# q and k of the first eight slots kept as one f32 tile each, their scores as one f32 product per head in row tiles, and the engines' lists of steps laid anew

## What is computed

```
x = x + attention(layernorm(x), Wqkv, Wo)      16 heads of 32, causal, softmax
x = x + ffn(layernorm(x), w1, w3, w2)          hidden size 1365
attention: scores = q k^T / sqrt(32); a = softmax(masked scores); o = a v; o Wo
ffn:       h1 = x w1q^T; h3 = x w3q^T; (silu(h1) * h3) w2q^T
           with wq = clip(round(w / mean|w|), -1, 1) * mean|w|
```

## Time and profile before

| | |
|---|---|
| median of the runs | 579.03 us (578.77 to 580.35, 3 runs) |
| the profiled execution, its own time | 580.78 us |
| its span in the profile | 579.0 us |
| mean granted TensorE clock | 0.941 of full speed |
| PE busy | 508.0 us (88%), 4092 matmuls |
| DVE, POOL, ACT busy | 411.8 us (71%), 368.4 us (64%), 330.2 us (57%) |
| first and last f16 score matmul | 37.1 and 472.8 us |
| scores of slot 5's first fill | 162.4 us |
| last phase (feed-forward of batch 3) | from 515.9 us on |

### The profile page before, as it was taken

How to read it: one execution, slowest core, us unless ns; L and a number is a source line. 1 busy time by engine, 2 the same in 40 slices (tenths; PEclk the granted TensorE clock), 3 DMA queues, 4 the chain that set the end, 5 groups by cost and what they waited for, 6 DMA issues and landing times.

```text
span 579.0 us, 11497 instructions
## 1 busy us (share of the span) xinstructions
PE 508.0 (88%) x4092; PEld 237.9 (41%) x4092; DVE 411.8 (71%) x1026; ACT 330.2 (57%) x833; POOL 368.4 (64%) x460
## 2 busy tenths in 40 slices
PE   2669754857999999999999999999999998839997
PEld 2224322333445444544444444454444454314443
DVE  6599787697899877966888879578878771523421
ACT  4769866777756875645467875363666752012320
POOL 3077689777968976776667887556668782312320
PEclk9689955878999999999999999999999999869999
DMA  8939978999889756387596565675783548030001
GB/s 312 316 30 278 193 170 160 252 200 211 153 141 162 145 124 131 56 158 194 108 167 143 90 131 97 141 180 114 101 173 75 109 87 208 9 63 1 0 37 72
DMA packets 224205, 79.52 MB, mean 137 GB/s; under 512 B 213226, under 2 KB 213226, under 8 KB 224148
## 3 DMA queue, kind: packets, MB, share of 16 engines
q1 hardware_dynamic: 224148, 78.79, 65.0%
HBM read 20.97 MB, written 4.19 MB: 43 GB/s over the span
## 4 chain that ended last, share of the span: by engine, by line
PE 69%; POOL 9%; DMA 8%; SPq 5%; DVE 4%; issue 2%; ACT 2%; DVEq 0%; ACTq 0%
PE work L1120 46%; PE work L1280 13%; DMA early<-early 4%; PE work L1239 4%; PE score_bank L1197 4%; POOL early L654 4%; PE work L1210 2%; DMA rows<-in_L_attn_x 2%; POOL late L687 2%; POOL early L687 1%; SPq L517 1%; DVE early L986 1%; DMA w_ternary<-early 1%; POOL rows L669 1%; DMA late<-rows 1%
## 5 line engine op out<-in xcount | busy, mean ns | idle before, releaser
L654 POOL TENSOR_TENSOR early<-early 128x512 f16<-128x512 f32 (+1 forms) x192 | 193.7, 1021 | 40.4 <-DVE early L986 26.5
L762 ACT ACTIVATE early<-early,exp_bias 128x512 f32<-128x512 f32 (+3 forms) x256 | 140.8, 551 | 76.7 <-POOL exp_bias L661 76.5
L1120 PE MATMUL work<-late,w_ternary 128*128 128x512 f16 (+1 forms) x704 | 158.9, 384 | 10.3 <-DMA late<-rows 10.3
L974 DVE CUSTOM_DVE_ANT_0 early<-score_bank,mask,scalars 128x512 f32<-128x512 f32 (+3 forms) x256 | 131.7, 543 | 32.7 <-POOL early L654 20.4
L986 DVE CAST early<-early 128x512 f16<-128x512 f32 (+1 forms) x148 | 99.5, 690 | 18.1 <-ACT early L762 14.7
L1120 PEld LDWEIGHTS work<-late,w_ternary 128*128 128x128 f16 (+1 forms) x704 | 69.2, 101 | 93.9 <-issue 17.9
L1120 PE MATMUL work<-xt,wqkv_hi 128*128 128x512 f16 x256 | 80.7, 398 | 2.9 <-DVE wqkv_lo L936 2.0
L1280 PE MATMUL work<-w_ternary,late 128*128 128x512 f16 (+1 forms) x352 | 77.7, 379 | 0.0
L679 POOL TENSOR_TENSOR late<-late 128x512 f16<-128x512 f32 (+1 forms) x44 | 51.3, 1168 | 40.1 <-ACT late L799 39.4
L792 ACT ACTIVATE late<-work,scalars 128x512 f32<-128x512 f32 (+1 forms) x44 | 30.0, 682 | 53.0 <-DVE late L1027 36.1
L1120 PE MATMUL work<-xt,wqkv_lo 128*128 128x512 f16 x128 | 51.0, 398 | 0.0
(11 more groups left out here) (103 smaller groups left out, 702.4 us busy)
## 6 DMA issues: line engine op xcount, KB each, us to landing
rows<-in_L_attn_x SPq DMA_DIRECT2D x16, 256.0 KB, 3.0
x_res<-in_L_attn_x SPq DMA_DIRECT2D x12, 256.0 KB, 3.2
out_y<-x_res SPq DMA_DIRECT2D x12, 256.0 KB, 2.8
late<-in_L_ffn_w SPq DMA_DIRECT2D x4, 682.5 KB, 5.5
early<-in_L_ffn_w SPq DMA_DIRECT2D x3, 768.0 KB, 12.8
late<-in_L_ffn_w SPq DMA_DIRECT2D x3, 768.0 KB, 6.7
late<-in_L_attn_Wqkv SPq DMA_DIRECT2D x4, 512.0 KB, 7.2
late<-in_L_attn_Wqkv SPq DMA_DIRECT2D x1, 1024.0 KB, 9.8
```

Source lines behind the costliest of these rows:

```text
L654: pool.tensor_tensor(split_view(s, p, 1, h), raw_view(s, p, h), split_view(s, p, 0, h), ALU.subtract).then_inc(low_done, 1)
L762: last = act.activation(piece, piece, ACT.Exp, bias=bias, accum_out=sums[:, s % 2, at:at + 1])
L974: last = dve.tensor_tensor_reduce(raws[n % RAWS][:, off:off + cols], score_bank[h][:, off:off + cols], mask[:, S - cols:S], scalar(exp_sca ...
L1120: last = pe.matmul(bank, lhs, rhs, start=(n == 0), stop=(n == len(terms) - 1))
```

## The change

For slots 0 to 7 (`WHOLE = 8`) ACT copies q and k once, as f32, into a whole tile; DVE makes no low half of them, and the bank is freed by ACT's copy. `scores` then issues one f32 product per head and piece in place of three f16 ones. The f16 halves of slots 8 to 15 lie in the same memory. `HALF` leaves out the copies without a partner, and `xt` on SP waits for the last reader in each work bank. The core of the diff:

```diff
@@ -42,6 +42,7 @@
 WARM = 4
 HALVES = 3
 RAWS = 4
+WHOLE = 8
 
 
 FILLS = (((3, 0, 512),), ((2, 0, 384), (0, 384, 128)), ((1, 0, 256),))
@@ -264,7 +272,8 @@
 
 
 WORK = numbered("pe", "top_turn", "weight_mean", "xt", "q", "k", "v", "project", "gate", "lin", "down", "inverse", "values")
-HALF = numbered("act", "xt", "yt", "q", "k", "v")
+HALF = {step: n for n, step in enumerate(s for s in ORDER["act"] if s[0] in ("xt", "yt", "v") or
+                                         s[0] in ("q", "k") and s[1] >= WHOLE)}
 HIGHS = {engine: numbered(engine, "high") for engine in ("act", "dve")}
 SPLIT = numbered("act", "split", "wo_split")
 
@@ -334,8 +343,9 @@
 
         v_hi = sb("v_hi", [P, ST, D], F16)
         v_lo = sb("v_lo", [P, ST, D], F16)
-        half = {(n, part_): [sb(f"{n}_{part_}{i}", [P, S], F16) for i in range(HALVES)]
-                for n in "qk" for part_ in ("hi", "lo")}
+        whole = {n: [sb(f"{n}{i}", [P, S], F32) for i in range(HALVES)] for n in "qk"}
+        half = {(n, part_): [w[:, at // 2:(at + S) // 2].bitcast(F16) for w in whole[n]]
+                for n in "qk" for part_, at in (("hi", 0), ("lo", S))}
 
         row_max = sb("row_max", [P, 2, 2 * HG], F32)
         exp_bias = sb("exp_bias", [P, 2, 2 * HG], F32)
@@ -544,8 +554,10 @@
                 kind, b, i = step
                 n = kind[0]
                 if kind == "xt":
-                    for used in [(m, GROUPS * b - 1) for m in "qk"] + [("v", b - 1, j) for j in range(ST)]:
-                        full(sp, used)
+                    readers = [(m, GROUPS * (b - 1) + g) for m in "qk" for g in range(GROUPS)]
+                    readers += [("v", b - 1, j) for j in range(ST)]
+                    for n_bank in range(NW):
+                        full(sp, max((r for r in readers if bank_of(r) == n_bank), key=turn_of))
                     sp.wait_ge(rows_split[n], ST * (b - 1) + i + 1)
                 else:
                     if b:
@@ -742,7 +754,11 @@
                 if s >= HALVES:
                     act.wait_ge(score_full, NF * (s - HALVES + 1))
                 full(act, step)
-                act.activation(half[n, "hi"][s % HALVES][:], work[bank_of(step)][:], ACT.Copy,
+                if s < WHOLE:
+                    act.activation(whole[n][s % HALVES][:], work[bank_of(step)][:], ACT.Copy,
+                                   scale=QK_SHRINK).then_inc(work_free[bank_of(step)], 1)
+                    return
+                act.activation(half[n, "hi"][s % HALVES], work[bank_of(step)][:], ACT.Copy,
                                scale=QK_SHRINK).then_inc(half_done, 1)
 
             def v_high(step):
@@ -952,7 +968,7 @@
                 n, s = step
                 bank = bank_of(step)
                 dve.wait_ge(half_done, HALF[step] + 1)
-                dve.scalar_tensor_tensor(half[n, "lo"][s % HALVES][:], work[bank][:], QK_SHRINK, half[n, "hi"][s % HALVES][:],
+                dve.scalar_tensor_tensor(half[n, "lo"][s % HALVES], work[bank][:], QK_SHRINK, half[n, "hi"][s % HALVES],
                                          ALU.mult, ALU.subtract).then_inc(work_free[bank], 1)
 
             def v_low(step):
@@ -1188,15 +1204,19 @@
                 if p == 0:
                     for n in "qk":
                         emptied(pe, (n, s))
+                at = s % HALVES
+                terms = [(half["q", a][at], half["k", b][at]) for a, b in (("hi", "hi"), ("hi", "lo"), ("lo", "hi"))]
+                if s < WHOLE:
+                    terms = [(whole["q"][at], whole["k"][at])]
                 for j, (tile, off, cols) in enumerate(FILLS[p]):
-                    for t, (a, b) in enumerate((("hi", "hi"), ("hi", "lo"), ("lo", "hi"))):
+                    for t, (q, k) in enumerate(terms):
                         for h in range(HG):
                             if fill and j == t == 0:
                                 pe.wait_ge(score_free, HG * (fill - 1) + h + 1)
                             heads = slice(HD * h, HD * (h + 1))
                             last = pe.matmul(score_bank[h][:, off:off + cols],
-                                             half["q", a][s % HALVES][heads, tile * P:(tile + 1) * P],
-                                             half["k", b][s % HALVES][heads, 0:cols], start=(t == 0), stop=(t == 2))
+                                             q[heads, tile * P:(tile + 1) * P], k[heads, 0:cols],
+                                             start=(t == 0), stop=(t == len(terms) - 1))
                 last.then_inc(score_full, 1)
 
             def inverse_rows(step):
```

All five lists are laid anew. The places of them that the prediction speaks of (lines before with -, lines after with +, cut at the sides by "..."):

```diff
     "sp":
-        x_load:1,1 res_load:0,2 res_load:0,1 x_load:1,0 weight_turn:w1,0 res_load:0,0 weight_turn:w1,1
-        weight_load:w3,0 weight_turn:w1,2 weight_load:w3,1-2 probs_turn:0,0 weight_load:w3,3 probs_turn:0,1 xt:1,0-1
+        x_load:1,0-1 weight_turn:w1,0 weight_load:w3,0-2 weight_turn:w1,1-2 weight_load:w3,3 res_load:0,2
+        probs_turn:0,0-2 xt:1,0-1 x_load:1,2-3 probs_turn:1,0 weight_load:w2,0 probs_turn:1,1 weight_turn:w3,0
     "pool":
-        bias:0,0,3 low:0,0,1-2 bias:0,1,1 low:0,0,3 bias:0,1,3 stats_x:1,1 low:0,1,0-3 bias:0,2,1 xt:1,0 low:0,2,0
-        bias:0,2,3 low:0,2,1-2 xt:1,1 bias:1,0,1 low:0,2,3 bias:1,0,3 low:1,0,0-2 bias:1,1,1 low:1,0,3 stats_x:1,2
-        bias:1,1,3 low:1,1,0-1 xt:1,2 stats_x:1,3 low:1,1,2-3 weight_round:w3,0 bias:1,2,1 weight_round:w3,1
+        low:0,0,2 bias:0,1,1 low:0,0,3 bias:0,1,3 low:0,1,0-2 bias:0,2,1 low:0,1,3 stats_x:1,1 low:0,2,0 bias:0,2,3
+        weight_round:w3,0 low:0,2,1-2 bias:1,0,1 low:0,2,3 weight_round:w3,1-2 xt:1,1 bias:1,0,3 low:1,0,0-1
+        weight_round:w3,3 low:1,0,2 bias:1,1,1 weight_round:w3,4 low:1,0,3 stats_x:1,2 weight_round:w3,5 bias:1,1,3
     "act":
-        split:2 weight_sum:w1,3 split:3 split:8 split:4 k:0 q:0 weight_ternary:w1,0 split:5 weight_ternary:w1,1-2
+        weight_sum:w1,2 split:2 weight_sum:w1,3 split:3 norm_x:1,0 split:8 weight_ternary:w1,0 k:0
+        weight_ternary:w1,1 q:0 split:4 weight_ternary:w1,2 split:5 weight_ternary:w1,3 split:6 weight_ternary:w1,4
     "dve":
-        pad:w1 stats_x:0,0-3 top_part:0-1 xt:0,0 top_part:2-3 xt:0,2-3 top_turn:qk top_v split:0 xt:0,1 top_turn:v
-        split:1 stats_x:1,0 split:2-3 weight_mean:w1 split:8 q:0 split:4 k:0 wo_max max:0,0,0 split:5 max:0,0,1
-        split:6 q:1 max:0,0,2 high:0,0,0 max:0,0,3 split:7 high:0,0,1 q:2 max:0,1,0 high:0,0,2 max:0,1,1 high:0,0,3
+        pad:w1 stats_x:0,0-3 top_part:0-3 xt:0,1 xt:0,0 xt:0,2 top_turn:qk xt:0,3 split:0 top_v stats_x:1,0 split:1
+        top_turn:v weight_mean:w1 wo_max split:2-3 split:8 split:4 max:0,0,0 split:5 max:0,0,1 split:6-7 v:0,0
+        max:0,0,2-3 high:0,0,0-1 top_turn:wo high:0,0,2 max:0,1,0-1 high:0,0,3 pad:w3 max:0,1,2-3 v:0,1 high:0,1,0-1
     "pe":
-        lin:2,10 values:14 down:2,0 scores:15,2 down:2,1-2 inverse:15 down:2,3 values:15 project:3,0-3 gate:3,0-1
+        values:14 scores:15,2 down:2,0-2 inverse:15 values:15 down:2,3 project:3,0-3 gate:3,0-1 lin:3,0-1 gate:3,2-3
```

More of the change, by code:

```diff
@@ L130 @@
+        low:14,1,0 lin:2,4 low:14,1,1-2 bias:14,2,1 low:14,1,3 lin:2,5 bias:14,2,3 low:14,2,0-2 lin:2,6 bias:15,0,1
+        low:14,2,3 bias:15,0,3 lin:2,7 low:15,0,0 lin:2,8 low:15,0,1-3 bias:15,1,1 lin:2,9 ot:13 bias:15,1,3
+        low:15,1,0 lin:2,10 low:15,1,1-2 bias:15,2,1 low:15,1,3 bias:15,2,3 low:15,2,0-3 ot:14-15 stats_y:3,0-1
+        yt:3,0-1 stats_y:3,2-3 yt:3,2-3 lin:3,0-10
     """,
     "act": """
-        norm_x:0,0-2 xt:0,0 norm_x:0,3 xt:0,1-3 weight_sum:w1,0 split:0 weight_sum:w1,1 split:1 weight_sum:w1,2
@@ new lines @@
+        stats_x:3,1 down:0,0 max:8,0,0 inverse:7 max:8,0,1-3 q:10 high:8,0,0-2 max:8,1,0 high:8,0,3 down:0,1
+        max:8,1,1-2 down:0,2 values:7 high:8,1,0 max:8,1,3 high:8,1,2 down:0,3 high:8,1,1 high:8,1,3 project:1,0
+        stats_y:1,0 max:8,2,0-1 project:1,1 max:8,2,2 stats_y:1,1 max:8,2,3 norm_y:1,0-1 v:2,0 project:1,2 max:9,0,0
+        stats_y:1,2 max:9,0,1-2 project:1,3 high:9,0,0 max:9,0,3 norm_y:1,2 stats_y:1,3 high:9,0,1 q:11 inverse:8
+        max:9,1,0 norm_y:1,3 max:9,1,1 high:9,0,2 v:2,1 high:9,0,3 k:11 max:9,1,2 v:2,2 max:9,1,3 v:2,3 high:9,1,0
@@ new lines @@
+        high:11,0,1 inverse:10 q:12 high:11,0,2 gate:1,10 max:11,1,0 q:13 max:11,1,1 lin:1,10 high:11,0,3 max:11,1,2
+        k:12 max:11,1,3 high:11,1,1 high:11,1,0 values:10 max:11,2,0 high:11,1,2 max:11,2,1 high:11,1,3 max:11,2,2
+        k:13 max:11,2,3 down:1,0 inverse:11 max:12,0,0 down:1,1 max:12,0,1-3 high:12,0,0-1 down:1,2 high:12,0,2
+        max:12,1,0 values:11 max:12,1,1-2 high:12,0,3 high:12,1,0 down:1,3 max:12,1,3 high:12,1,1 project:2,0
+        max:12,2,0 stats_y:2,0 high:12,1,2-3 max:12,2,1-2 project:2,1 norm_y:2,0 max:12,2,3 stats_y:2,1 project:2,2
@@ new lines @@
+        high:14,1,0 gate:2,5 high:14,1,1 lin:2,5 max:14,2,0 high:14,1,2 values:13 max:14,2,1 high:14,1,3 gate:2,6
+        lin:2,6 max:14,2,2-3 gate:2,7 lin:2,7 max:15,0,0-1 inverse:14 max:15,0,2 gate:2,8 max:15,0,3 lin:2,8
```

(18 more changed lines are left out.)

259 lines of the change are left out of this document (116 added, 143 removed).

## The result

The change makes the kernel slower by 0.3 to 0.6 per cent: 581.85 us median (580.74 to 583.15) against 580.01 us (577.64 to 580.65), eight runs each, ratio 1.0046 with a 95% interval of 1.003 to 1.0063. The ratios here are not the quotients of the medians, which can differ from them by some 0.1%. Run again beside other kernels it gave 581.66 us, 1.005 (1.0032 to 1.0067). The forecast, 570.8 us, had the wrong sign, and its range (562 to 579) does not hold the result.

A forecast was written before the change was run, and what follows sets the result against it. It saw a front of waits between four engines, a stretch bound by TensorE's matmuls, and an end with a stall. Terms -2.0 + 1.9 - 3.5 - 4.6 = -8.2 us gave 570.8 us against the median, range 562 to 579.

The forecast's parts named there:

- start -2.0: Start: x_load 1,0 issued first and w1's mean read earlier, so w1's rounding begins about 2.0 us earlier; first scores at 34 us.
- front -3.5: Front up to scores 5,0: less DVE work plus DMA room used, less the late w1 turn (1 us), gives -3.5 us.
- f32 +0.5: Front's f32 score fills: +2.9 us of matmuls, of which 0.5 us was put on the path.
- +1.4: Eight f32 score fills in the saturated stretch (5,1 to 7,2): four tiles abreast, 4/3 of the passes, +1.4 us.
- -4.6: End: down 2,3 behind values 15 removes the 2.85 us ot_lo stall and 1.7 us of half clock: -4.6 us.
- the price put on DVE's time: Front: of 9.5 us less DVE work, at most a third, 2 to 3 us, reaches a waiting engine.
- Rival 3: Front is held by DMA and POOL whatever DVE does; the last 3.5 us do not come, 574.5 us; 20%.
- the 2.5 us for the new order's use of DMA: Front: w3 loads issued earlier, while DMA has room, gain about 2.5 us net of the residual loads.
- Rival 4: Front loses: late w1 turn or new POOL list delays biases; front +3 instead of -5.5, 579 us or more; 11%.
- The mark: TensorE time of a 512-column f32 fill: 0.9 to 1.0 us forecast, 2.1 shows rival 2, 3.4 rival 1.
- rivals 1 and 2: f32 row tiles run one at a time (592 us, 7%), or half overlapped, two heads' records together (579 us, 6%).
- moved waits on SP cost nothing: SP's moved waits of xt cost nothing, as TensorE is past those matmuls in both orders.

The follow-up runs named there:

- e3: Kernel before with its lists, DVE's q and k steps of slots 0 to 7 struck out, three products of hi halves alone: 578.41 us, 0.9996.
- e2: Changed kernel with its own lists, but scores of slots 0 to 7 as three f16 products of hi halves, no f32: 582.17 us, 1.0063.
- e4: Kernel before with only down 2,3 moved behind values 15 on TensorE, its DVE step ahead of project 3,0: 577.05 us, 0.997.
- e7: Changed kernel with first scores ahead of q:1 on TensorE and split 1 ahead of the statistics of x 1,0 on DVE: 581.82 us, 1.0055.
- e12: Changed kernel with two low halves of v moved up on DVE: 581.38 us, 1.0039.
- e6: Changed kernel with w1's three turns on SP ahead of the first three w3 loads: 585.34 us, 1.0108.
- e1: Changed kernel's f32 product on the engine lists of the kernel before, DVE's q and k steps of slots 0 to 7 struck out: 582.47 us, 1.007.
- e8: Lists of the kernel before with the end of e4, f32 product for slots 0 to 4 only (WHOLE = 5): 578.45 us, 0.9981.
- e10: e8 with f32 for all eight slots (WHOLE = 8), DVE's q and k steps of slots 5 to 7 struck out: 580.18 us, 1.0017.
- e5: Changed kernel with batch 0's turned rows of y ahead of slot 4's last probability turn and xt 2,0 on SP: 583.12 us, 1.0057.
- e9: Changed kernel with w2's last two chunks rounded, signed and turned earlier, and e5's order on SP: 582.33 us, 1.0066.

## Why the prediction was wrong

**The prediction's sum, against the balance.** Both are counted against the profiled execution of before.

| stretch | predicted | profiled |
|---|---|---|
| up to scores 5,0 | -5.0 (start -2.0, front -3.5, f32 +0.5) | +1.9 (matmuls +4.1, lost -2.3) |
| f32 fills after it | +1.4 | +2.5 |
| new wait, scores 5,0 to 6,0 | none | +2.6 lost |
| scores 6,0 to 15,0 | none | -1.0 lost |
| end up to gate 3,0 | -4.6 | -3.4 lost |
| after gate 3,0 | none | -1.3 lost |
| sum | -8.2 | +1.3 |

**The failed step is the front's -3.5**, both of its gains. The first is the price put on DVE's time, 2 to 3 us. The prediction read 20.6 us of waits for row_max as a sign that a third of DVE's saved time would reach a waiting engine. e3 shows that none does, within 1.3 us. A wait names who came last. It does not say that this engine's own work was what the others were short of. Rival 3 (20%), by which the front does not care what DVE does, was right on that; its time, 574.5 us, failed with the other terms. The second is the 2.5 us for the new order's use of DMA: by medians the new lists without their end cost an estimated 5.8 us when there is no f32 product (3.8 of e2 less e3, and e4's 2.0), of which about 3 us lie at gate 0,0 (below) and the rest in the front.

**The front's new order costs instead of giving.** From the chain of the changed kernel's whole span:

```profile
48.77 3.11 SPq L614
...
51.93 3.81 DMA w_ternary<-early
...
55.75 8.55 DMA early<-early
...
82.85 5.01 POOL early L666 x4
...
87.93 6.29 SPq L580
...
94.26 2.09 SPq L614
...
106.10 8.45 DMA early<-early
```

w1 is turned at 55.7 us (53.2 before, forecast 54 to 55), and the first probability turn lands at 64.3 us. That is not earlier than before: the piece of the earlier trace rows that ends at 69.5 us is two turns. DVE's cast behind the first one starts, in the kernel before and then in the changed one, at

```profile
61.21 0.29 DVE L986 CAST early<-early 128x256 f16<-128x256 f32 x1 [0.27 <-DMA early<-early]
```

```profile
64.32 0.29 DVE L1002 CAST early<-early 128x256 f16<-128x256 f32 x1 [1.59 <-DMA early<-early]
```

By issue and time to landing, slot 0's three turns land at 64.3, 70.4 and 73.6 us (61.2, 69.5 and 75.9 before) and slot 1's first at 89.2 (86.1). The first three w3 loads do land 5 us earlier (52.2 us, 57.3 before), but of the turns only the third gained by it. Behind them the chain has low halves on POOL, 8.4 us of SP issuing two transposes (87.93, probabilities, and 94.26, the first of w3's turns, which SP issued at 118.65 us before), and DMA that is at 0.98 in the window from 80 to 100 us. Meanwhile scores 1,0 start 4.8 us later than before, behind v_lo and the w1 turn. But e7, which has the first scores 4.6 us earlier, and e12, which has scores 1,0 1.8 us earlier, gain nothing, and neither did e3 by relieving DVE. What is left is the ring of POOL, SP and DMA; that the front hangs on it is argued from the chain, and which of its new neighbours there costs the most was not tried one by one. Rival 4 (the front loses, 11%) had the place and may have half of the mechanism: the late w1 turn does hold DVE up (2.45 us), but turning w1 first makes w3 late instead, which is worse (e6).

**The start's -2.0 came and was lost at once.** The load of x 1,0 landed at 26.5 us (29.1 before) and DVE read w1's mean at 28.8 us, earlier than the 29.5 forecast. But the first scores came at 38.0 us, not 34. The same chain, a little earlier:

```profile
13.31 13.21 DMA rows<-in_L_attn_x
...
28.45 5.02 PE work L1136 x12
...
35.25 2.76 PE work L1136 x12
38.01 1.07 PE score_bank L1217 x8
```

k:0 waited 3.5 us for split 1 and started at 28.45 us, as forecast. But the granted clock had fallen (0.58 from 28 to 34 us, 1.00 from 34 to 38), and its 12 matmuls took 5.02 us where q:1's took 2.76; and q:1 stood ahead of the scores and waited 1.8 us for a bank. The prediction overlooked these two. e7 undid them and gained nothing, so the first scores were never what the front hung on.

**The f32 fill: mechanism right, size off.** (This is the +1.4, which measured 2.2 us over the same eight fills.) The mark was 0.9 to 1.0 us against 2.1 and 3.4 for the rivals. It is 1.07, so four f32 tiles run abreast and rivals 1 and 2 are refuted. The term counted 4/3 of the passes, 0.42 ns more per column. That holds, but each fill also has a fixed part over its passes at 2.4 GHz: 1.07 - 0.85, 1.08 - 0.85 and 0.64 - 0.43 are 0.21 to 0.23 us, where the f16 fills have 0.12 to 0.13 (0.76 - 0.64, 0.77 - 0.64, 0.44 - 0.32). So +0.1 us a fill was missing, 0.8 over the eight. The loads, by shape, against the earlier trace rows:

```profile
L1217 PEld LDWEIGHTS score_bank<-k,q 32*128 32x128 f32 x256 | 17.7, 206 | 26.1 <-DVE row_max L990 12.7 <-issue 7.9 <-ACT q L758 3.8
...
L1217 PEld LDWEIGHTS score_bank<-k,q 32*128 32x128 f16 x384 | 7.4, 92 | 11.5 <-issue 8.9
```

The fixed parts are near one weight load of each kind (0.206 and 0.092 us). That is a reading of the numbers, and no run shows it. What the fills show is that a second piece pays no more: the 384+128 fill has two and takes 1.08 us. The Trainium skill, page "TensorE: Matmul & The Clock Gate", section "Weight-path perf modes", says that the fast weight load is not used for FP32; the rows agree so far as an f32 load takes 2.2 times as long. The prediction set the packing figure of the same page of the Trainium skill (an estimated 1.11 us a fill) aside for the neighbouring rows' 0.97, and the page was nearer to the 1.07 measured.

The 0.5 us for f32 in the front is neither confirmed nor refuted: scores 5,0 start 0.2 us earlier in e1's profile than in e3's, the medians leave 1.6 us (e1 and e3) and 1.4 us (e8 and e4).

**The missing term: a wait of 2.9 us at gate 0,0.** The prediction let moved waits on SP cost nothing and never priced the turned rows of y. From the same chain, later on:

```profile
172.84 1.27 SPq L569
...
174.21 3.28 DMA late<-rows
...
177.51 1.30 DVE rows L898
...
179.54 1.17 POOL rows L681
...
180.78 4.08 DMA late<-rows
...
185.12 5.34 PE work L1136 x24
```

SP issues these rows at 172.8 us, 5.2 us later than before (167.7), and gate 0,0 starts at 185.1, not 180.1. These turns wait in the program until w2 is turned, and SP issues w2's last two turns, from 166.78 us on, only just ahead of them:

```profile
166.78 3.20 SPq L611 DMA_TRANSPOSE w_ternary<-late  x2
```

The lists make most of the wait and not f32: on the new lists it is 3.0 us without f32 (e2), on the old lists 0.3 us without (e3) and 1.3 to 1.5 us with f32 (e1, e8, e10). But e5 and e9 show that SP's order and w2's place are not enough to remove it (e9, with w2 turned by 164.3 us, still waits 2.8 us): behind them stand the statistics and the normalisation of y. Moving those too was not tried, so its last cause stays open.

**The end: right in kind, one size off.** The wait for ot_lo is gone and project 3's first 24 matmuls run at the full clock, 5.20 us for 7.04. What the prediction denied is that values 15 would wait for its probabilities. e4's chain, around the end of slot 15:

```profile
477.44 1.95 POOL early L654 x3
479.45 4.46 DMA early<-early
...
484.04 1.82 PE work L1239 x57
485.86 4.86 PE work L1280 x22
490.72 5.20 PE work L1120 x24
```

In e4 values 15 waits 1.9 us on that transpose, and 1.5 us in the changed kernel. Moving scores 15,2 earlier on TensorE (in the changed kernel, not in e4) did not make their turn earlier: from their first matmul to the landing of the turn 17.2 us pass in the changed kernel and 12.9 in e4, as exp, POOL's low half and the transpose follow their own lists. -4.6 became -3.4 by the balance of the changed kernel and -2.7 by e4's, and e4's median is 2.0 us below the kernel before (its profile, its fastest run, 5.5 us). The step needs neither f32 nor new lists. The table's last -1.3 us is no part of it: the 176 matmuls of 512 columns that open the last phase, partly at half clock, take 39.5 us in the changed kernel and in e4, but 40.8 us in the kernel before and in e8, which has e4's end. No run ties that to the change.
